# Cross-attention with a routed feed-forward layer on one core: the ranks, the turn of x and the turn of the shift change their places and PSUM banks in the attention slots

## The reference

```
xn = layernorm(x)                                  # over the 128 features
q = xn @ Wq.T;  k, v = split(ctx @ Wkv.T)          # 16 heads of 8
att = softmax(where(mask, q.k / sqrt(8), -1e9))
x = x + (att @ v) @ Wc.T
xf = layernorm(x);  logits = xf @ router.T         # 8 experts
top 2 of 8, probs = softmax(top values)
out = x + sum over the 2 experts of prob * (gelu(xf @ w1[e].T + b1[e]) @ w2[e].T + b2[e])
```

## Time and profile before

| what | value |
|---|---|
| median of 3 runs | 385.14 us (384.53 to 386.89) |
| profiled execution | span 383.3 us, mean granted PE clock 0.959; its own time outside the span is not recorded |
| busy, share of the span | PE 309.2 us (81%), DVE 255.3 (67%), POOL 241.7 (63%), ACT 232.6 (61%) |
| DVE's maxima, L1315 | 87.0 us in 128, with 34.8 us of idle time before them until PE's scores L1040 |
| POOL's row sends, L706 | 63.5 us in 64, with 16.8 us of idle time before them until DVE L1444 |
| chain that ended last | PE 45%, POOL 21%, issue 14% |
| FFN matmuls, L1235 and L1244 | 77.8 and 77.0 us |

### The profile page before, as it was taken

How to read it: one execution, slowest core, us unless ns; L and a number is a source line. 1 busy time by engine, 2 the same in 40 slices (tenths; PEclk the granted TensorE clock), 3 DMA queues, 4 the chain that set the end, 5 groups by cost and what they waited for, 6 DMA issues and landing times.

```text
span 383.3 us, 11559 instructions
## 1 busy us (share of the span) xinstructions
PE 309.2 (81%) x3720; PEld 251.8 (66%) x3720; DVE 255.3 (67%) x750; ACT 232.6 (61%) x566; POOL 241.7 (63%) x387
## 2 busy tenths in 40 slices
PE   1633878998997979797988089999999999999930
PEld 0211546666666657475765079889999999998930
DVE  7406678889788889788868826785545554556752
ACT  1311366879787878877788037556666666666520
POOL 7796335352487786858486786577877666665550
PEclk9999989999999999999999559999999999999995
DMA  5589454566474463442110386575986766669846
GB/s 152 93 212 232 130 138 114 145 111 175 124 201 129 146 170 101 130 130 58 36 54 31 96 262 185 167 223 163 275 239 196 232 202 208 204 172 353 271 119 192
DMA packets 61850, 62.95 MB, mean 164 GB/s; under 512 B 14109, under 2 KB 46260, under 8 KB 61632
## 3 DMA queue, kind: packets, MB, share of 16 engines
q1 hardware_dynamic: 55168, 50.34, 48.6%
q0 software_dynamic: 4320, 8.47, 6.4%
q10 hardware_dynamic: 2304, 3.41, 2.8%
HBM read 37.65 MB, written 11.88 MB: 129 GB/s over the span
## 4 chain that ended last, share of the span: by engine, by line
PE 45%; POOL 21%; issue 14%; DVE 7%; DMA 5%; SPq 4%; ACT 2%; DVEq 0%; POOLq 0%; ACTq 0%
PE sexp L1244 16%; PE smax L1235 15%; POOL dispatch_d L706 10%; PE smax L1040 3%; SPq L443 3%; DVE shift L1315 2%; PE tail L1084 2%; POOL rstd L666 2%; POOL qpart L619 2%; DMA stacks<-result_d 1%; DMA kmask<-mask_dram 1%; POOL shift L626 1%; PE feed L1031 1%; PE feed L1016 1%; POOL xq L614 1%
## 5 line engine op out<-in xcount | busy, mean ns | idle before, releaser
L1315 DVE TENSOR_REDUCE shift<-smax 128x4 f32<-128x512 f32 x128 | 87.0, 684 | 35.8 <-PE smax L1040 34.8
L792 POOL DMA_INDIRECT result_d<-y_out,stacks x71 | 70.7, 995 | 31.3 <-issue 29.5
L706 POOL DMA_INDIRECT dispatch_d<-rows_out,row_i x64 | 63.5, 993 | 34.2 <-DVE rows_out L1444 16.8
L871 ACT ACTIVATE probs<-sexp 128x512 f32<-128x512 f32 x128 | 74.2, 592 | 10.1 <-PE sexp L1048 9.1
L1235 PE MATMUL smax<-probs,w_ring 128*128 128x128 f32 x568 | 77.8, 281 | 1.6 <-ACT probs L978 1.0
L1244 PE MATMUL sexp<-w_sb,probs 128*128 x568 | 77.0, 279 | 2.6 <-ACT probs L982 2.4
L1768 DVE TENSOR_TENSOR probs<-smax,b_cols 128x512 f32<-128x512 f32 x71 | 49.1, 691 | 42.4 <-PE smax L1235 38.5
L1244 PEld LDWEIGHTS sexp<-w_sb,probs 128*128 128x128 f32 x568 | 69.8, 194 | 5.0 <-issue 4.9
L1235 PEld LDWEIGHTS smax<-probs,w_ring 128*128 128x128 f32 x568 | 70.7, 196 | 3.3 <-issue 2.9
L982 ACT ACTIVATE probs<-probs 128x512 f32<-128x512 f32 x71 | 44.8, 631 | 37.6 <-DVE probs L1768 37.5
L1040 PE MATMUL smax<-stacks 64*128 64x128 bf16 x512 | 47.9, 225 | 12.9 <-DMA stacks<-kpart 7.0
(11 more groups left out here) (215 smaller groups left out, 511.4 us busy)
## 6 DMA issues: line engine op xcount, KB each, us to landing
w_ring<-w_t_dram SPq DMA_DIRECT2D x71, 256.0 KB, 3.6
stacks<-kpart SPq DMA_DIRECT2D x48, 128.0 KB
stacks<-qpart SPq DMA_DIRECT2D x48, 128.0 KB
stacks<-dispatch_d SPq DMA_DIRECT2D x71, 65.0 KB, 3.5
stacks<-result_d ACTq DMA_DIRECT2D x12, 256.0 KB, 4.4
ctx<-ctx_t_dram SPq DMA_DIRECT2D x8, 256.0 KB, 3.7
w_sb<-w_t_dram SPq DMA_DIRECT2D x8, 256.0 KB, 3.4
out_dram<-xw SPq DMA_DIRECT2D x8, 256.0 KB, 3.3
```

The costliest lines, as they stand in the source:

```text
L706: nc.gpsimd.indirect_dma_start(out=dispatch_d, out_offset=bass.IndirectOffsetOnAxis(ap=row_i[r % RR][:, k, b:b + 1], axis=0), in_=rows_out ...
L792: nc.gpsimd.indirect_dma_start(out=result_d, out_offset=bass.IndirectOffsetOnAxis(ap=xg[r][:, D + 1:D + 2].bitcast(U32), axis=0), in_=y_ou ...
L871: nc.scalar.activation(dst, sexp[hp][:], ACT.Exp).then_inc(exp_done, 1)
L1315: nc.vector.tensor_reduce(shift4[n % 2][:, hp, 0, 4 * m:4 * m + 4], smax[hp][:], AX.X, ALU.max, negate=True).then_inc(max_taken, 1)
```

## The change

The ranks of all rounds now go into columns 256 to 287 of the attention bank `tail`, and are issued after the third set of scores and the shift turn; the wait for the attention copy takes the place of the waits for the splits. The turn of x goes into the bank `feed` at the end of the slot before the one in which it was, ahead of `project_y`; ACT's copy of it stays in its slot and place, and reads `feed`. The turn of the shift goes from before `turn_y` to behind the third scores, and waits for ACT's copy of y; ACT's copy of the shift goes from before `copy_yt` to behind exp 2.

```
-XT_AT = GB + 1
+XT_AT = GB
-        rank_ps = [(tail if r == ROUND - 1 else feed)[:, 0:GB * EXPERTS] for r in range(ROUND)]
+        rank_ps = tail[:, 2 * SEQ:2 * SEQ + GB * EXPERTS]
@@ ACT
-            def copy_shift(n, p):
+            def copy_shift(n):
                 act.wait_ge(shift_turned, n + 1)
-                if p is not None:
-                    act.wait_ge(yt_done, p + 1)
...
-                nc.scalar.activation(x_t[:], heads[:], ACT.Copy).then_inc(xt_copied, 1)
+                nc.scalar.activation(x_t[:], feed[:], ACT.Copy).then_inc(xt_copied, 1)
...
-                if turning(s) is not None:
-                    copy_xt(turning(s))
+                if turning(s - 1) is not None:
+                    copy_xt(turning(s - 1))
                 if 0 <= a < BATCH:
                     copy_attn(a)
-                if 0 < s <= BATCH:
-                    copy_shift(s - 1, p if p >= 0 else None)
                 if 0 <= p < BATCH:
                     copy_yt(p)
...
                 if 0 <= e < BATCH:
                     exp(e, 2)
+                if 0 < s <= BATCH:
+                    copy_shift(s - 1)
@@ PE
             def turn_shift(n, p):
...
-                if p is not None and p > 0:
-                    pe.wait_ge(resid_done, p)
+                if p is not None:
+                    pe.wait_ge(yt_copied, p + 1)
...
-            def turn_x(g, n):
-                pe.wait_ge(y_ready, n)
+            def turn_x(g):
+                pe.wait_ge(v_copied, g + 1)
+                pe.wait_ge(q_split, 4 * min(g + 2, GROUPS - 1) + 2)
                 for b in range(GB):
-                    last = nc.tensor.transpose(heads[:, b * SEQ:(b + 1) * SEQ], xs[:, GB * g + b, :], ident)
+                    last = nc.tensor.transpose(feed[:, b * SEQ:(b + 1) * SEQ], xs[:, GB * g + b, :], ident)
...
             def turn_y(n):
                 if n:
                     pe.wait_ge(resid_done, n)
+                else:
+                    pe.wait_ge(shift_copied, LAG + 1)
...
                 scores(m, e, 0)
-                if turning(s) is not None:
-                    turn_x(turning(s), min(a, BATCH))
...
                 scores(m, e, 1)
-                r = routing(s, 3)
-                if r is not None:
-                    if r == 0:
-                        pe.wait_ge(ranks_set, 2)
-                    pe.wait_ge(q_split, 4 * min(r + 4, GROUPS - 1) + 2)
-                    if r == FIRST_ROUNDS:
-                        pe.wait_ge(table_steps, 1)
-                    elif r == FIRST_ROUNDS - 1:
-                        pe.wait_ge(v_copied, GROUPS)
-                    rank(r)
                 if 0 <= a < BATCH:
...
+                    if routing(s, 4) is not None:
+                        routed(pe, routing(s, 4), RANKS_STEP)
                     attend(a)
+                if 0 <= p < BATCH:
+                    turn_y(p)
+                scores(m, e, 2)
                 if 0 < s <= BATCH:
...
-                    turn_shift(s - 1, p if p >= 0 else None)
-                if 0 <= p < BATCH:
-                    turn_y(p)
-                scores(m, e, 2)
+                    turn_shift(s - 1, p if 0 <= p < BATCH else None)
+                r = routing(s, 3)
+                if r is not None:
+                    if r == 0:
+                        pe.wait_ge(ranks_set, 2)
+                    pe.wait_ge(attn_copied, min(a + 1, BATCH))
+                    rank(r)
...
-                    if g >= 3:
-                        routed(pe, g - 3, RANKS_STEP)
+                    else:
+                        pe.wait_ge(xt_copied, g)
                     project_v(g)
...
                 if 0 <= a < BATCH:
...
-                    if turning(s) is not None:
-                        pe.wait_ge(xt_copied, turning(s) + 1)
                     turn_heads(a)
+                if turning(s) is not None:
+                    turn_x(turning(s))
                 if 0 <= p < BATCH:
                     project_y(p)
```

More of the change, by code:

```diff
@@ L1121, in rank @@
                     pe.wait_ge(carried, r)
-                nc.tensor.matmul(rank_ps[r], before[:], picked[:, batches(r), :].rearrange("p b e -> p (b e)"), start=True, stop=False)
+                nc.tensor.matmul(rank_ps, before[:], picked[:, batches(r), :].rearrange("p b e -> p (b e)"), start=True, stop=False)
                 for j in range(1, GB):
                     own = picked[:, GB * r:GB * (r + 1) - j, :].rearrange("p b e -> p (b e)")
-                    nc.tensor.matmul(rank_ps[r][:, j * EXPERTS:], ones_b[:], own, start=False, stop=False)
-                nc.tensor.matmul(rank_ps[r], ones_b[:],
+                    nc.tensor.matmul(rank_ps[:, j * EXPERTS:], ones_b[:], own, start=False, stop=False)
+                nc.tensor.matmul(rank_ps, ones_b[:],
                                  carry[:, r, :].rearrange("p (o e) -> p o e", o=1).to_broadcast([P, GB, EXPERTS]),
@@ L1171, in _ @@
                 scores(m, e, 1)
+                if 0 <= a < BATCH:
+                    if a == 0:
+                        pe.wait_ge(k_split, 6)
+                    if routing(s, 4) is not None:
+                        routed(pe, routing(s, 4), RANKS_STEP)
+                    attend(a)
+                if 0 <= p < BATCH:
+                    turn_y(p)
+                scores(m, e, 2)
+                if 0 < s <= BATCH:
+                    if s == 1:
+                        pe.wait_ge(q_split, 2)
+                    turn_shift(s - 1, p if 0 <= p < BATCH else None)
                 r = routing(s, 3)
@@ L1205, in _ @@
                     pe.wait_ge(carried, FIRST_ROUNDS)
-                    routed(pe, FIRST_ROUNDS - 1, RANKS_STEP)
+                    pe.wait_ge(xt_copied, GROUPS)
                     nc.tensor.matmul(first_total_ps, ones_b[:], carry[:, FIRST_ROUNDS, :], start=True, stop=True).then_inc(total_done, 1)
@@ L1406, in row_ranks @@
                 dve.wait_ge(ranks_done, r + 1)
-                nc.vector.tensor_tensor(tmp8[i][:], rank_ps[r].rearrange("p (b e) -> p b e", b=GB),
+                nc.vector.tensor_tensor(tmp8[i][:], rank_ps.rearrange("p (b e) -> p b e", b=GB),
                                         first_row[:].rearrange("p (o e) -> p o e", o=1).to_broadcast([P, GB, EXPERTS]),
```

## The result

The changed kernel took **389.02 us** (median of 6 runs, 388.05 to 391.13) beside 384.87 us for the kernel before (6 runs, 383.88 to 386.89): ratio 1.0103, 95% interval 1.0073 to 1.0134. A repetition gave 1.0101 [1.0062, 1.0141]. The forecast was 385.2 with a range to 388.5, so it missed by 3.8 us; slower by over 1% had been given a chance of 0.08.

What follows compares the result with a forecast made beforehand. No engine was full: attention slots were a ring of waits, PE's stream longest. About +0.4 us to slot 25, then POOL-led slots giving most back, summed to +0.1: 385.2 us, range 382.5 to 387.9, with rival parts 381.5 to 388.5.

Steps and rivals of the forecast that it cites:

- The walk: Attention slots 6 to 36, followed instruction by instruction for what each slot kind gains or loses; +0.1 us in all.
- D slot: Every fourth slot (s modulo 4 = 3, queries): -0.35 us, +0.13 in slots 7 and 11, -0.5 in slot 15.
- C: Slots with s modulo 4 = 2 (keys): new wait 0.13 us, +0.25 in all.
- B: Slots with s modulo 4 = 1 (values, formerly turn of x): values start 2.47 us after second scores against 2.10, +0.37.
- A slots: Slots with s modulo 4 = 0 (ranks): -0.41 us to the second scores of B; +0.24 in slot 8.
- the short one named as a sign: At L1073, the shift turn: a short wait for ACT's y_t in nearly every slot instead of POOL's.
- Sum to slot 25: Slot terms from slot 6 to the second scores of B at slot 25, together about +0.4 us.
- rival 2: ACT's order becomes the bound in the slots: y copy 0.2 us later, +5.4 us, 391 us; chance 0.12.
- Rival 1: PE's 12.2 us of stalls really go, 373 us, or a third of it, about 381; chance 0.20.
- Rival 3: Nothing moves: POOL's sends from slot 25 set the start of the FFN, 385.1 us; chance 0.10.
- Rival 4: DVE's rank steps meet a POOL send in each of six groups: +2.4 us, 387.6 us; chance 0.08.
- The covers: Slack on SP, POOL and DVE hides the moved shift copy, ranks and residual; a failure costs about 1 us a group.

Runs made afterwards that it cites:

- wait-filled row: Changed kernel with the third transposed scores written five times more before the shift turn in slots 8, 12, 16, 20, 24: 386.79 us, 1.0041.
- fast version: Changed kernel with the shift turned into the heads bank, waiting for DVE's y instead of ACT's copy of y: 382.06 us, 0.9898.
- the last kernel above: Changed kernel with the shift turned into the heads bank and x early, but ranks in their old place and feeding bank: 383.17 us, 0.9946.
- x alone: Kernel before with only the turn of x moved one slot ahead into the feeding bank: 382.77 us, 0.9935; on the slower chip 416.64, 0.9964.

## Why the prediction was wrong

**The walk was right.** L1123 and L1091 stand without idle time, L1071 waits for ACT's y_t in nearly every slot. In slot 16 the fourth scores come at 121.55 behind the D slot's fourth scores at 116.06: 5.49 us, forecast 139.93 - 134.52 = 5.41. The waits of C and D slots were 0.17 to 0.18 (forecast 0.13), of B 0.41 where no fall came before it. Only the wait of the A slots was not the short one named as a sign. ACT's y copy in slot 16, the step on which all rested:

```profile
120.49 0.37 ACT L860 ACTIVATE attn_t<-tail 128x256 f32<-128x256 f32 x1
120.76 0.28 ACT L876 ACTIVATE y_t<-prep 128x128 f32<-128x128 f32 x1
```

It ends at 121.04, 4.98 us behind the D slot's fourth scores; forecast 139.47 - 134.52 = 4.95. The wait-filled row of the table, which has no fall, follows the walk: a loss of 1.76 at slot 25 (forecast 0.76), most of it given back by slot 29 (-1.19, forecast about -0.8), +0.35 in the end (forecast +0.1). Its groups of four slots take 21.35 us, forecast 21.15 within 0.3.

**The step that failed** is the term of the A slot in "Sum to slot 25": -0.41 was worked out with every duration behind the stand taken from rows at full clock. The walk implied the stand, though it never wrote it down: the shift at 139.53, TensorE there at 137.57 - 1.27 + 1.60 = 137.90, so 1.6 us (measured 1.73), and it counted this only as time. In two of four groups the clock fell to 0.5 behind it for 3.4 us, and the term became about +0.9 (-0.41 + 1.32, an estimate): 1.32 and 1.36 us, together 2.7, by the trace; 2.3 in the medians, where filling the stand took them away. The forecast's own range, with "0.1 us of error a slot", had no place for such a jump, and none of the rivals priced the clock. The sign for rival 2, a period over 21.8 us, was met in the two groups with a fall (22.66 and 22.71; the others 21.35 and 21.47), but by the clock and not by ACT's order.

**The second part is what the sum left out: slots 0 to 5.** It began at slot 6, but the changed kernel is 1.15 us behind there already, 0.58 when repeated. Over all traces of this study the state at slot 5 lies between -1.10 and +2.08. The late ones (+0.43 and over) have a stretch at 0.5 just ahead of or in slot 5, or a longer one before it; those on time have a short one earlier. There are two exceptions: the last kernel above (-1.10) and x alone on the slower chip (-0.03), each with a fall just ahead of or in slot 5. PE also waits 2.8 us for DVE's shift from 40 to 66 us, but the fast version waits 2.3 and is early. What sets this part stays open; 0.6 to 1.2 us of the loss lie in it.

**By the terms.** Taking the filled version as the walk without falls, 3.19 from slot 5 on is +0.35 and a rest of +2.84, of which the two falls are 2.7; the 1.15 before it makes 4.3. The repetition gives +0.35, +2.48 and +0.58.

**The wait was worth more than I priced beside it.** I set the wait against the stalls that go, and both came out even: +0.1. Without the wait the two other moves and the later shift gain 2.75 us from slot 5 to 36. So the even sum was 2.75 gained and about 3.1 lost by standing, before any fall; with the wait put back in the same bank it was 4.2.

**Rivals.** Rival 1 (a third of the stalls goes, 381) describes the version in the heads bank, 382.1, and not the change. Rival 2 gave the nearest time, 391, but by another mechanism: its condition, a y copy ending later than 139.9 - 134.52 = 5.4 us behind the D slot's fourth scores, was not met (4.98). Rival 3 is out: first transposes from 216.90 to 225.73 show that the start of the FFN follows the slots. Rival 4 went the other way: the casts of the row numbers in slots 13, 17, 21 and 25 took 0.16 to 0.39 us in the changed kernel, for 0.53 to 0.97 before (the earlier trace rows has the last, which ends at 164.55 with POOL's operation at 164.53). The covers held: DVE stands up to 1.3 us for the ranks (L1404, 5.5 us in five rounds), and PE's list of waits above has none for DVE.

## What to carry to other kernels

A stand of TensorE can have two prices: the time, and the clock behind it. Three waits (1.3, 0.7, 0.4 us) gathered into one of 1.7 lost more here than they saved, and the three moves together cost what none of them cost alone. So measure the parts, but do not add them; and where the sum of a walk is near zero, look at the longest single stand that it makes and price the next stretch at the lower clock as a rival of its own. And before a moved instruction is made to wait for the neighbours of its PSUM bank, look for a bank that another part of the same change has just left free: here that was the difference between 1.0% slower and 1.0% faster.

## What the runs showed of the hardware

- The granted clock fell to 0.5 for some 3.4 us behind stands of 1.73 us in two of four groups (one of four in the heads bank), behind stands of 1.28 us in two of four, and once each behind 0.95, 1.00, 1.07 and 1.34 us in three other versions; it stayed at 1.00 behind twenty stands of 1.27 to 1.32 us in five versions, and with stands of 0.6. While it was down, 32 attention matmuls took up to 1.93 us in place of 1.08, and a slot of the changed kernel 1.3 us more. Which stands were followed by a fall differed between two executions of one kernel; no run settles why.
- 20 small matmuls more in each of five slots made the changed kernel 2.3 us faster and the kernel before 3.7 us slower.
- One chip ran the kernel before in 419.17 us where two others took 385; for one and the same variant, 19.0 us of the difference lay ahead of the FFN stage and 13.3 in it. The shift's move alone cost 3.3% there and 0.6% on an ordinary chip.
